# Cross-attention and a soft mixture of experts on one core: the last combine shift shared by two engines, its scale in quarters on VectorE, and two pieces of work placed elsewhere

## The reference

```python
x = x + xattn(layernorm(x), ctx_1024)          # 16 heads of 64, softmax over 1500 keys
logits = (einsum('tzd,ed->tze', layernorm(x), phi_w) + phi_b).reshape(t, z, 64, 32)
D = softmax(logits, axis=3)                    # dispatch: over the 32 slots of an expert
C = softmax(logits, axis=2)                    # combine: over the 64 experts
X_tilde = einsum('tznp,tzd->npd', D, x)        # the 2048 slots
X_tilde = tanh(normalised(clip(X_tilde, -33000, 65000)))
Y_tilde = einsum('npd,ndH->npH', X_tilde, expert_w) + expert_b[:, None, :]
x = x + einsum('tznp,npH->tzH', C, Y_tilde)
```

## Time and profile before

| what | value |
|---|---|
| median of three runs | 447.81 us |
| profiled execution, its own time | 448.28 us |
| its span | 446.5 us |
| TensorE busy | 428.5 us, 96% |
| VectorE busy | 338.2 us, 76% |
| ACT busy | 246.2 us, 55% |
| GpSimd busy | 138.5 us, 31% |

### The profile page before, as it was taken

How to read it: one execution, slowest core, us unless ns; L and a number is a source line. 1 busy time by engine, 2 the same in 40 slices (tenths; PEclk the granted TensorE clock), 3 DMA queues, 4 the chain that set the end, 5 groups by cost and what they waited for, 6 DMA issues and landing times.

```text
span 446.5 us, 7523 instructions
## 1 busy us (share of the span) xinstructions
PE 428.5 (96%) x3038; PEld 391.6 (88%) x3038; DVE 338.2 (76%) x618; ACT 246.2 (55%) x421; POOL 138.5 (31%) x76
## 2 busy tenths in 40 slices
PE   2899999999999999999999999999999999899997
PEld 2788899999999999889999998989999888798986
DVE  2567777786786767767898688988997999668871
ACT  2366555665565456645664665636755654633641
POOL 2509000503050005030704053255340343446740
PEclk9999999999999999999999999999999999999999
DMA  8162200111011001110110011000100001476000
GB/s 215 62 157 22 71 19 12 21 63 18 13 16 67 19 12 20 64 18 13 13 70 19 12 13 69 19 1 15 13 18 3 10 13 31 82 196 182 1 3 21
DMA packets 15110, 19.05 MB, mean 43 GB/s; under 512 B 3954, under 2 KB 10882, under 8 KB 15076
## 3 DMA queue, kind: packets, MB, share of 16 engines
q1 hardware_dynamic: 14788, 17.53, 16.1%
q10 hardware_dynamic: 288, 1.05, 0.8%
HBM read 18.32 MB, written 0.26 MB: 42 GB/s over the span
## 4 chain that ended last, share of the span: by engine, by line
PE 78%; DVE 10%; ACT 5%; DMA 2%; issue 2%; POOL 2%; POOLq 1%; ACTq 0%
PE turned L626 15%; PE scores L614 8%; PE acc L648 8%; PE acc L647 8%; PE acc L646 8%; PE scores L616 8%; PE scores L615 8%; PE misc L663 3%; PE misc L551 3%; DVE small L1226 2%; PE misc L688 2%; DVE pT_l L1236 2%; PE misc L545 2%; ACT prob L1002 2%; DMA wk_sb<-in_L_xattn_Wk_dram 2%
## 5 line engine op out<-in xcount | busy, mean ns | idle before, releaser
L995 ACT CAST pT_h<-turned 125x512 fp32r<-125x512 f32 x168 | 94.9, 589 | 122.5 <-PE turned L626 121.8
L1236 DVE TENSOR_TENSOR pT_l<-turned,pT_h 125x512 fp32r<-125x512 f32 x168 | 112.2, 687 | 59.5 <-ACT pT_h L995 59.0
L1226 DVE TENSOR_REDUCE small<-scores 128x1 f32<-128x500 f32 x168 | 109.2, 674 | 11.2 <-PE scores L616 11.0
L626 PE MATMUL turned<-ident,prob 128*125 128x128 f32 x672 | 94.7, 276 | 2.9 <-DVE pT_l L1236 2.6
L626 PEld LDWEIGHTS turned<-ident,prob 128*125 128x125 f32 x672 | 87.4, 187 | 10.6 <-DVE pT_l L1236 4.3
L646 PE MATMUL acc<-pT_h,ctx_nh 125*128 125x256 f32 (+1 forms) x288 | 94.6, 329 | 0.0
L1002 ACT ACTIVATE prob<-scores,small 128x1500 f32<-128x1500 f32 x56 | 84.9, 1516 | 13.4 <-DVE small L1229 13.4
L648 PE MATMUL acc<-pT_h,ctx_nl 125*128 125x256 f32 (+1 forms) x288 | 86.5, 300 | 0.0
L647 PE MATMUL acc<-pT_l,ctx_nh 125*128 125x256 f32 (+1 forms) x288 | 86.3, 300 | 0.0
L614 PE MATMUL scores<-ctx_th,qk_h 128*128 128x500 f32 x168 | 68.2, 406 | 1.9 <-DVE qk_l L1219 1.2
L616 PE MATMUL scores<-ctx_th,qk_l 128*128 128x500 f32 x168 | 65.3, 389 | 0.0
(11 more groups left out here) (164 smaller groups left out, 536.8 us busy)
## 6 DMA issues: line engine op xcount, KB each, us to landing
ctx_raw<-in_ctx_dram SPq DMA_DIRECT2D x7, 750.0 KB
rbc<-rden_row SPq DMA_DIRECT2D x15, 128.0 KB, 3.2
rbc<-rden_row SPq DMA_DIRECT2D x8, 192.0 KB, 3.2
eb<-in_L_ffn_expert_b_dram SPq DMA_DIRECT2D x4, 256.0 KB, 5.8
ctx_raw<-in_ctx_dram SPq DMA_DIRECT2D x3, 250.0 KB
wq_sb<-in_L_xattn_Wq_dram ACTq DMA_DIRECT2D x1, 512.0 KB, 4.8
wk_sb<-in_L_xattn_Wk_dram ACTq DMA_DIRECT2D x1, 512.0 KB, 8.7
wv_sb<-in_L_xattn_Wv_dram SPq DMA_DIRECT2D x1, 512.0 KB, 9.4
```

Source lines behind the costliest of these rows:

```text
L626: last = tr(turned[0:CK, m, 128 * c:128 * c + 128], prob[u][:, CK * j:CK * j + CK], ident[:, :])
L995: nc.scalar.copy(pT_h[0:CK, PLACES[g // NT % 2][t], CPB * k:CPB * k + CPB, :], turned[0:CK, (KB * u + k) % 2, :].rearrange("p (c r) -> p c ...
L1226: m = v.tensor_reduce(bankmax[:, u, k:k + 1], scores[:, k, 0:KW], AX.X, ALU.max)
L1236: v.tensor_tensor(pT_l[0:CK, place, dst, :], turned[0:CK, (KB * u + k) % 2, :].rearrange("p (c r) -> p c r", c=CPB), pT_h[0:CK, place, dst ...
```

## The change

Four edits, all at or behind the last attention tile.

1. `dispatch_exp(2)` on ACT moves from batch 7, tile 6, to behind the three copies of the last tile, and `copy_last_rbc` moves behind the third copy. On VectorE `lo_probs` of the last tile's first bank moves ahead of `normalise(7, 1)`.
2. On TensorE `slots_in(0, 2)` moves ahead of the wait for the copied `x2n`; the other slot products of pairs 0 and 1 move up by one place.
3. The upper half of `combine_shift(LAST)` moves from GpSimd to VectorE, behind `slot_stats(2)`. ACT's `combine_exp(LAST)` waits for both halves and moves ahead of `tanh_slots(2)`.
4. The whole of the last combine scale runs on VectorE in four quarters, and `turn_comb(LAST)` waits for each. Of VectorE's bias adds the second moves ahead of `slot_stats(3)`, the third behind both sums.

```diff
             def combine_shift(q, n0=0, n1=N_EXP):
@@ gpsimd
             slot_root(1)
             combine_shift(LAST, 0, N_EXP // 2)
             slot_root(2)
-            combine_shift(LAST, N_EXP // 2, N_EXP)
             slot_root(3)
-            combine_scale(LAST, QUARTER)
@@ tensor
             def turn_comb(q):
-                pe.wait_ge(comb_pool, q + 1)
+                if q < LAST:
+                    pe.wait_ge(comb_pool, q + 1)
                 for r in range(4):
-                    if q == LAST and r == 1:
-                        pe.wait_ge(comb_dve, 1)
+                    if q == LAST:
+                        pe.wait_ge(comb_dve, r + 1)
...
             turn_x2n(LAST, M0)
+            slots_in(0, 2)
             pe.wait_ge(x2nT_act, NQ)
             for c in range(LC):
                 pe.wait_ge(combT_act, 4 + c + 1)
                 logits(LAST, c)
-                if c > 0:
-                    slots_in(0 if c < 3 else 1, c + 1 if c < 3 else 0)
-                if c == 0:
+                if c == 1:
+                    slots_in(0, 3)
                     pe.wait_ge(disp_pool, 2)
+                if c > 1:
+                    slots_in(1, c - 2)
             pe.wait_ge(disp_pool, 3)
             for r in range(4):
-                if r > 0:
+                if r > 1:
                     slots_in(1, r)
@@ scalar
             def combine_exp(q):
-                act.wait_ge(csub_pool, NQ + 1 if q == LAST else q + 1)
+                act.wait_ge(csub_pool, q + 1)
+                if q == LAST:
+                    act.wait_ge(csub_dve, 1)
...
-                if b == B - 1 and t == 6:
-                    dispatch_exp(2)
...
             hi_probs(G - 1, 1, NT - 1, 1)
+            hi_probs(G - 1, 1, NT - 1, 2)
             copy_last_rbc()
-            hi_probs(G - 1, 1, NT - 1, 2)
+            dispatch_exp(2)
             combine_exp(2)
...
             copy_xtT(1)
+            combine_exp(LAST)
             tanh_slots(2)
-            combine_exp(LAST)
@@ vector
             invert(B - 1, 2)
+            lo_probs(G - 1, 1, NT - 1, 0)
             normalise(B - 1, 1)
-            lo_probs(G - 1, 1, NT - 1, 0)
...
-            def combine_scale_upper(q):
+            def combine_shift_upper(q):
+
+                half_n = slice(N_EXP // 2, N_EXP)
+                dve.wait_ge(cmax_dve, q + 1)
+                v.tensor_tensor(by_expert(comb[q][:, :])[:, half_n, :], by_expert(logit[q][:, :])[:, half_n, :],
+                                cmax[q][:, :].unsqueeze(1).broadcast_to([PT, N_EXP // 2, P_SLOT]),
+                                ALU.subtract).then_inc(csub_dve, 1)
+
+            def combine_scale_quarter(q, r):
 
                 dve.wait_ge(crec_dve, q + 1)
-                upper = by_expert(comb[q][:, QUARTER:])
-                v.tensor_tensor(upper, upper, csum[q][:, :].unsqueeze(1).broadcast_to([PT, 3 * N_EXP // 4, P_SLOT]),
+                part = by_expert(comb[q][:, QUARTER * r:QUARTER * r + QUARTER])
+                v.tensor_tensor(part, part, csum[q][:, :].unsqueeze(1).broadcast_to([PT, N_EXP // 4, P_SLOT]),
                                 ALU.mult).then_inc(comb_dve, 1)
...
             slot_stats(2)
+            combine_shift_upper(LAST)
             dve.wait_ge(eb_in, 16 * EPT)
             add_expert_bias(0)
+            add_expert_bias(1)
             slot_stats(3)
-            add_expert_bias(1)
             combine_sum_part(LAST, 0)
+            combine_sum_part(LAST, 1)
             add_expert_bias(2)
-            combine_sum_part(LAST, 1)
-            combine_scale_upper(LAST)
+            for r in range(4):
+                combine_scale_quarter(LAST, r)
             add_expert_bias(3)
```

More of the change, by code:

```diff
@@ L446, in dispatch_scale, with combine_scale @@
                                  ALU.mult).then_inc(disp_pool, 1)
-            def combine_scale(q, end=SLOTS):
+            def combine_scale(q):
                 pool.wait_ge(crec_dve, q + 1)
-                part = comb[q][:, 0:end].rearrange("p (n s) -> p n s", s=P_SLOT)
-                gp.tensor_tensor(part, part,
-                                 csum[q][:, :].unsqueeze(1).broadcast_to([PT, end // P_SLOT, P_SLOT]),
+                gp.tensor_tensor(by_expert(comb[q]), by_expert(comb[q]),
+                                 csum[q][:, :].unsqueeze(1).broadcast_to([PT, N_EXP, P_SLOT]),
                                  ALU.mult).then_inc(comb_pool, 1)
```

## The result

The changed kernel takes 446.22 us (median of 20 runs, 445.33 to 448.51); the kernel before took 447.88 in 20 runs (447.02 to 449.85). The ratio is 0.996, 95% interval 0.995 to 0.9971: 1.7 us of gain. The prediction said 446.0, range 444.9 to 447.9.

What follows compares the result with a forecast made beforehand. Bound: mostly TensorE matmuls (78% of the chain); the edits act on the path to TensorE's last two late starts. Gain 0.19 + 1.49 + 0.1 = 1.8 us gives 446.5 profiled, 446.0 median; range 444.9 to 447.9.

Steps and rivals of the forecast that it cites:

- Part 1: Last attention tile: with the dispatch exponential behind the copies, the projection starts 0.88 us earlier; bounds 0 and 1.17.
- Part 2: First logits: a slot product fills 0.34 us of TensorE idleness but overhangs, a loss of 0.34 us; bounds 0 and 0.6.
- there it had waited for nobody, so that is worth nothing by itself: End of the slots: TensorE gains the filled idleness there, but this was claimed to be worth nothing.
- Part 3: Shared shift: VectorE's half waits for GpSimd's, ending at 421.99; the earlier exponential lets `combine(0, 2)` start 0.19 us earlier.
- Rival (a): Shared shift: VectorE and GpSimd don't exclude each other, upper shift ends 0.52 earlier; gain 2.3, time 445.5; chance 0.14.
- Rival (b): Shared shift: GpSimd's small operations retake the port, VectorE waits 1.95 us; time 447.95; chance 0.10.
- Part 4: Last combine scale: VectorE's quarters remove TensorE's 1.49 us idleness before the last transposes, with 0.1 of record overlap.
- by half a microsecond: Bias add before `combine(0, 2)`, behind both sums: VectorE is free at 429.4, the experts end at 429.9.
- Rival (c): Head: the projection stays at 393.71, so 0.88 us is missing and the time is 446.9; chance 0.15.
- The gain over 0.5%: Whole kernel: measured faster by over 0.5%, below 445.57 us; chance 0.32.

Runs made afterwards that it cites:

- The run with half of it: Kernel before with the last dispatch exponential moved behind the copies, VectorE's order left alone: 447.2 us, ratio 0.999.
- without the quarters: Changed kernel with GpSimd scaling the first quarter again and VectorE the rest in one instruction, new bias-add order kept: 446.2 us, ratio 0.9954.
- part 3 undone: Changed kernel with both shift halves on GpSimd and the combine exponential behind the third tanh group, new bias-add order kept: 447.71 us, ratio 1.0001.
- the two runs on part 1: Edit 1 undone in the changed kernel: 447.34 us, 446.97 when run again; edit 1 alone on the kernel before: 446.64 us.
- part 1 undone: Changed kernel with the dispatch exponential, reciprocals' copy and normalise(7, 1) back in their old places: 447.34 us, ratio 0.9971; run again 446.97, ratio 0.9972.
- quarters alone: Kernel before with the last combine scale in four quarters on VectorE, bias adds in the old order: 446.72 us, ratio 0.9972.
- part 2 alone: Kernel before with only the slot products moved up, the first ahead of the wait for x2n: 447.38 us, ratio 1.0001.
- the border at 24: Changed kernel with GpSimd shifting 24 of 64 experts instead of 32 and VectorE the rest: 446.0 us, ratio 0.9957.
- the border at 16: Changed kernel with GpSimd shifting 16 of 64 experts instead of 32 and VectorE the rest: 445.91 us, ratio 0.9956.

## Why the prediction was right, and where its ledger was not

**Part 1** came as worked out. The third turn stands at 2.33 (384.86 - 382.53; predicted 386.0 - 383.66 = 2.34), the dispatch sums hold `normalise(7, 2)`, and 0.92 us reach the projection (predicted 0.88); alone the edit takes 0.85 off the end. The run with half of it shows that the swap on VectorE was needed for a third of that.

**Part 2** has the predicted size, 0.92 - 0.55 = 0.37 at VectorE's first maximum and 0.33 at the end in the changed kernel. The reason I gave was wrong as it stood: "there it had waited for nobody, so that is worth nothing by itself". In the kernel before VectorE's 1.57 us of idleness in the earlier trace rows were a wait for just this TensorE work, and I had read that very number to find when VectorE is free. It holds only once part 3 has filled the wait.

**Part 3**: the exclusion is shown, by the record of 1.71 against 1.73 for one and a half times the numbers. I had the instruction's own time at 1.22; it worked 1.09 behind GpSimd's end. Rival (a), no exclusion, is out. Rival (b), that GpSimd goes again before the waiting VectorE, is out for this place: VectorE, 0.62 us in waiting, went ahead of an operation that GpSimd recorded 0.09 after its previous one. Where the Trainium skill's page SBUF — State Buffer (section Who interferes with whom) has the two exclude each other for whole instructions, these traces agree.

I had read part 3 too kindly. By my own working VectorE is 0.54 us ahead up to the last combine maximum and `combine(0, 2)` only 0.19; measured are 0.55 and 0.22. Between these two places lies VectorE's half of the shift, which takes time from the bias adds.

**Part 4** is the step that failed, though the sum didn't. I booked the 1.49 us of pause to the quarters, because the row of the pause names GpSimd's scale as its end. The runs show that the scale had only to be done 1.5 us earlier, and that the rest of the change brings either form of it in time: 58.70 without the quarters, 58.71 with them. Part 3 starts the exponential 3.2 us earlier (38.32; 41.51 with part 3 undone), and both sums stand ahead of the third bias add. For that new order the prediction only asked whether VectorE is in time ("by half a microsecond"; it waited 0.61) and gave it no worth; by the estimate above it is needed to end the pause without the quarters.

Alone from before the parts give 0.85 (part 1), 0.33 (part 2) and 1.28 (quarters). Undone in the changed kernel they lengthen the tail by 0.84 (part 1), -0.33 (part 2), 1.46 (part 3) and -0.01 (quarters). Neither column sums to 1.77; part 3 and the order of the bias adds have no run by themselves. The total was right because I had followed one path from end to end and counted its pause once.

**Rival (c)**, the head gives nothing, is out by the two runs on part 1. The gain over 0.5%, to which I gave a chance of 0.32, didn't come: 1.7 us are 0.4%.

## What to carry to other kernels

Work a set of edits out as one path with all of them in place; a price for each edit holds only beside the others. Then do the same sum with each edit left out, the order of small instructions counted as one of them: here that sum would have put part 3 in doubt. Ask of every pause how many of the edits would end it alone, and of every "nobody waits for this" whether the idle row that you use for another purpose is that wait. Where VectorE and GpSimd share an element-wise job with both inputs in SBUF, put the border where the one ends as the other begins; it can be worked out from the two durations. Here that was 24 of 64 experts, the shortest tail of the three borders tried (58.73 at 16, 58.48 at 24, 58.71 at 32).

## What the runs showed of the hardware beyond that

**TensorE's clock fell to half behind short pauses, in some executions only.** In the first run with part 1 undone the clock fell to 0.50 for 3.4 us behind the pauses of 0.44 and 1.36 us, and the execution took 448.99 against a median of 446.97 for the same kernel later. Kernels that keep the 1.36 us pause had a mean granted clock under 1.00 in 21 of 131 executions (before 13 of 84, part 1 undone 2 of 23, quarters alone 3 of 12, part 2 alone 3 of 12), those without it in 2 of 81, each such execution some 2 us longer. The kernel with part 3 undone, which has no such pause at the head but one of 2.24 us later, had 4 of 12. This points to the pauses, and would be a gain of part 1 that no single profile shows. It isn't settled: the counts differ between the three sets of runs (the kernel before alone 8 of 28, 3 of 24 and 2 of 32), and only one fall behind the 1.36 us pause was seen in a profile. A second fall was seen in the kernel with the border at 24. It lasted 3.4 us too, from 18.8 to 22.2, and began with the matmuls behind another pause, one of 1.20 us that the kernels before and after have as well (at 18.64 and 17.51) without a fall in their profiles:

```profile
18.76 0.73 PE L611 MATMUL scores<-ctx_th,qk_h 128*128 128x500 f32 x1 [1.20 <-DVE qk_l L1219]
```

**The tail repeats to some 0.02 us.** `combine(0, 2)` stood at 46.99, 46.98 and 47.01 in three kernels (the changed one, without the quarters, with the border at 16) whose paths should be the same or 0.02 apart, while the position of the copy that I measure from varied between 382.51 and 384.27 where the clock stayed at 1.00. Distances within a profile settled differences of 0.2 us that medians of 5 to 12 runs could not.
